# One edge tile in four of layer 0 keeps its messages in one fp32 tensor instead of a high and a low part

## The reference, cut to what matters

```
msg  = relu(x[src] + edge_attr @ W_e + b_e)          # 21250 x 512, edge_attr 21250 x 64
aggr = segment_sum(msg, dst)                         # 1250 x 512
h    = (1 + eps) * x + aggr
h    = silu(batch_norm(h @ W1 + b1)); h = silu(batch_norm(h @ W2 + b2))
x    = layer_norm(x + h)
```

## Time and profile before

| | us |
|---|---|
| median of 3 runs | 876.99 (876.02 to 877.89) |
| the profiled execution, its own time | 880.07 |
| its span, first to last instruction | 878.2 |

### The profile page before, as it was taken

One profiled execution on the slowest core, in us unless ns is written; L12 is line 12 of the kernel. 1 busy time (PEld: TensorE's weight loads), 2 busy tenths in 40 slices (PEclk: granted clock), 3 DMA queues, 4 the chain that ended last, 5 costly groups with the idle time before them and its releaser, 6 DMA issues.

```text
span 878.2 us, 11402 instructions
## 1 busy us (share of the span) xinstructions
PE 793.8 (90%) x3714; PEld 628.5 (72%) x3714; DVE 655.6 (75%) x1161; ACT 450.3 (51%) x805; POOL 349.9 (40%) x381
## 2 busy tenths in 40 slices
PE   7398999898969999969679999999999999999993
PEld 6265655555539999958358888878767798989893
DVE  6379999999997973268569999999985362525365
ACT  4377888888864432211157778778753121111122
POOL 6356677777700000011487777777720000000001
PEclk8789999999999999979789999999999999999996
DMA  8759888888820031003668888888831210100011
GB/s 222 261 157 324 262 245 256 251 251 252 265 95 1 1 121 72 1 12 128 204 191 248 264 257 259 263 256 262 263 100 36 72 72 1 72 1 1 1 49 69
DMA packets 49293, 134.38 MB, mean 153 GB/s; under 512 B 8169, under 2 KB 8425, under 8 KB 48848
## 3 DMA queue, kind: packets, MB, share of 16 engines
q0 software_dynamic: 26720, 87.58, 33.1%
q1 hardware_dynamic: 22020, 45.59, 15.2%
q10 hardware_dynamic: 492, 0.45, 0.2%
HBM read 128.47 MB, written 5.12 MB: 152 GB/s over the span
## 4 chain that ended last, share of the span: by engine, by line
PE 62%; DVE 24%; issue 6%; DMA 4%; ACT 2%; POOL 1%; SPq 0%; DVEq 0%; ACTq 0%; POOLq 0%
PE banks L499 36%; PE banks L526 12%; DVE msg_lo L1085 8%; DVE raw L1093 5%; PE banks L552 4%; PE banks L553 4%; DVE attr_hl L1008 3%; DVE hot L1079 3%; DMA attr_sb<-in_attr 2%; DVE agg L1108 1%; PE banks L566 1%; DVE stats L1209 1%; DMA raw<-table_dram,src_sb 1%; PE banks L575 1%; POOL raw L428 1%
## 5 line engine op out<-in xcount | busy, mean ns | idle before, releaser
L428 POOL DMA_INDIRECT raw<-in_x,src_sb x167 | 159.0, 952 | 80.6 <-DVE msg_lo L1085 50.2
L428 POOL DMA_INDIRECT raw<-table_dram,src_sb x167 | 163.0, 976 | 63.7 <-issue 35.8
L552 PE MATMUL banks<-msg_hi,hot 128*128 128x512 f32 x334 | 142.0, 425 | 9.5 <-DVE msg_lo L1085 7.0
L450 POOL TENSOR_TENSOR moments<-moments,minus_half 128x1 f32<-128x1 f32 x32 | 20.3, 635 | 322.7 <-DVE moments L1215 322.7
L869 ACT ACTIVATE msg_hi<-raw 128x512 fp32r<-128x512 f32 x168 | 105.5, 628 | 69.2 <-DVE raw L1093 67.4
L553 PE MATMUL banks<-msg_lo,hot 128*128 128x512 f32 x334 | 132.6, 397 | 0.0
L1093 DVE TENSOR_TENSOR raw<-banks,raw 128x512 f32<-128x512 f32 x168 | 114.2, 680 | 16.1 <-PE banks L526 12.8
L1085 DVE SCALAR_TENSOR_TENSOR msg_lo<-banks,msg_hi 128x512 fp32r<-128x512 f32 x166 | 112.7, 679 | 15.8 <-ACT msg_hi L869 15.8
L830 ACT ACTIVATE banks<-raw 128x512 f32<-128x512 f32 x166 | 98.7, 595 | 44.5 <-DMA raw<-table_dram,src_sb 36.6
L1085 DVE SCALAR_TENSOR_TENSOR msg_lo<-raw,msg_hi 128x512 fp32r<-128x512 f32 x168 | 113.7, 677 | 3.3 <-ACT msg_hi L869 3.3
L552 PEld LDWEIGHTS banks<-msg_hi,hot 128*128 128x128 f32 x334 | 63.8, 191 | 52.6 <-DVE msg_lo L1085 42.9
(11 more groups left out here) (167 smaller groups left out, 1650.9 us busy)
## 6 DMA issues: line engine op xcount, KB each, us to landing
attr_sb<-in_attr SPq DMA_DIRECT2D x84, 128.0 KB, 4.6
attr_sb<-in_attr SPq DMA_DIRECT2D x42, 256.0 KB, 3.9
Wg_raw<-in_Wg SPq DMA_DIRECT2D x3, 1536.0 KB, 6.5
W_raw<-in_W SPq DMA_DIRECT2D x2, 2048.0 KB, 14.1
raw<-in_x,src_sb POOLq DMA_INDIRECT x167, 4.3
raw<-table_dram,src_sb POOLq DMA_INDIRECT x167, 4.1
x_in<-in_x SPq DMA_DIRECT2D x5, 512.0 KB, 10.4
rows<-in_x SPq DMA_DIRECT2D x1, 2560.0 KB, 12.4
```

What stands on the lines that cost most here:

```text
L428: pool.indirect_dma_start(rows_of(L, t), None, tables[L], bass.IndirectOffsetOnAxis(ap=src_sb[:, t:t + 1], axis=0)).then_inc(gathered[t % ...
L552: nc.tensor.matmul(acc, h, msg_hi[L][:, t % MSG, :], start=start, stop=False)
```

## The change

In layer 0, tiles 3, 7, 11, ... 163 (t % 4 == 3, 41 of 167, all of them odd) become "whole". ACT writes their relu as plain fp32 into `msg_whole`, which lies on the same bytes as layer 0's `msg_hi` and uses the same slots. DVE computes no low part for them. PE sums them with one product on fp32 operands, `hot` read as fp32, where it made two on fp32r operands. Semaphore `low` counts only the tiles that have a low part, and whoever waited for a whole tile's low part (`place` and `sum_product`) waits for its relu (`relued`). The waits of `gather` name even tiles, so their counts change and not what they wait for. Layer 1 is as before.

```
+        msg_whole = at("msg_whole", [P, MSG, D], F32, B0 + 68 * KB)
...
+        def whole(L, t):
+            return L == 0 and t % 4 == 3
+        def lows(L, tiles):
+            return len([t for t in range(tiles) if not whole(L, t)])
...
-                    pool.wait_ge(low[L], t - RAW + 1)
+                    pool.wait_ge(low[L], lows(L, t - RAW + 1))
...
-                pe.wait_ge(low[L], t + 1)
+                if whole(L, t):
+                    pe.wait_ge(relued[L], t + 1)
+                else:
+                    pe.wait_ge(low[L], lows(L, t + 1))
...
-                nc.tensor.matmul(acc, h, msg_hi[L][:, t % MSG, :], start=start, stop=False)
-                mm = nc.tensor.matmul(acc, h, msg_lo[L][:, t % MSG, :], start=False, stop=stop)
+                if whole(L, t):
+                    mm = nc.tensor.matmul(acc, h.bitcast(F32), msg_whole[:, t % MSG, :], start=start, stop=stop)
+                else:
+                    nc.tensor.matmul(acc, h, msg_hi[L][:, t % MSG, :], start=start, stop=False)
+                    mm = nc.tensor.matmul(acc, h, msg_lo[L][:, t % MSG, :], start=False, stop=stop)
...
-                    act.wait_ge(low[L], t - 2 * PLACE_BANKS + 1)
+                    last = t - 2 * PLACE_BANKS
+                    if whole(L, last):
+                        act.wait_ge(relued[L], last + 1)
+                    else:
+                        act.wait_ge(low[L], lows(L, last + 1))
...
+                to = msg_whole if whole(L, t) else msg_hi[L]
+                nc.scalar.activation(to[:, t % MSG, :], edge_bank(t) if odd(t) else rows_of(L, t),
...
-                        if 0 <= t < TILES:
+                        if 0 <= t < TILES and not whole(L, t):
                             low_message(L, t)
```

More of the change, by code:

```diff
@@ L868, in message_high @@
                 wait(act, summed[L], t - MSG + 1)
-                nc.scalar.activation(msg_hi[L][:, t % MSG, :], edge_bank(t) if odd(t) else rows_of(L, t),
+                to = msg_whole if whole(L, t) else msg_hi[L]
+                nc.scalar.activation(to[:, t % MSG, :], edge_bank(t) if odd(t) else rows_of(L, t),
                                      ACT.Relu).then_inc(relued[L], 1)
```

## The result

The changed kernel takes **870.93 us** (median of 6 runs, 866.74 to 872.91) where the kernel before, timed beside it, takes 877.3 (872.71 to 878.27): a ratio of 0.9926 with a 95% interval of 0.9901 to 0.995. It is faster by 6.4 us; 13.5 us were forecast, and 870.9 lies above the upper end of the range.

The account below looks back on a forecast made before the run. DVE was taken to bound layer 0's edge loop, POOL's gathers next. Gathers 8.4 us earlier plus a shorter end made 14.1; less 0.6, 13.5 off the median 876.99 gave 863.5 us, range 860.5 to 869.5.

Parts of the forecast that it names:

- DVE bounds the loop before: Layer 0's edge loop: DVE sets the pace at 1.31 us a tile, 1.16 after the change, and other engines wait.
- PE's product at 0.88 us: A whole tile's sum on PE: one fp32 product of 512 columns costs 0.88 us where two fp32r products cost 0.47.
- the three rivals on PE's price: Layer 0's loop: PE dearer (866 to 870 us, chance 0.12), PE full (873, 0.04), PE the bound (891, 0.05).
- 116 x 1.25 = 145.0: POOL's gathers, tile 50 to 166: 1.25 us each instead of 1.314, so the last gather starts 8.4 us earlier.
- layer 1's period: Layer 1's gathers: 15.16 us for 12 tiles instead of 15.0; used in layer 0, it would take off 1.6 us.
- The last gather to the last low part, 10.0 us: End of layer 0's loop: 10.0 us, from layer 1's 10.6 less one low part, where it was 15.7.
- Where the gain can begin: Layer 0 from about 85 us: tile 50's gather starts at 87.1 instead of 88.11, about 1.0 us earlier.
- The profile stands for the median: The 13.5 us gain read from the profiled execution (880.07 us) was taken off the median, 876.99 us.
- 14.1 forecast: Layer 0's last low part ends at 242.1 instead of 256.2 us, 14.1 us earlier, before 0.6 us is taken off.
- The rest after layer 0 moved unchanged: Everything behind layer 0's edge loop moves with the loop's end, with no change of its own.
- the gather rate falls: Rival, layer 0's loop: transfers stretch and land late, about 8 us gained less delays, 869 to 873 us; chance 0.05.
- ACT's `place` does wait for them: Sign in the second part of layer 0's loop: ACT's `place` waits for gathers, as in layer 1; no size given.

Follow-up runs that it names:

- before_d: The kernel before, unchanged, run again for a second profile without the long common pauses: 875.84 us, ratio 0.999.
- after_c: The changed kernel, run again on another chip without the long common pauses: 871.08 us, ratio 0.9935 to the kernel before.
- port_free_c: Changed kernel with one SBUF operand of DVE's one-hots, features' and even tiles' low parts read from idle PSUM (sums not the reference's): 866.04 us, ratio 0.9893.
- third and fourth sets: Follow-up runs with at most one common pause each: kernels before and after, variants of whole tiles, DVE operands and load order; medians 865.81 to 883.57 us.
- odd2: Changed kernel with all odd tiles of layer 0 whole, 83 instead of 41: 957.45 us (ratio 0.986) with pauses, 883.57 us (1.0083) without.

## Why the prediction was wrong

The pair `before_d` and `after_c` fits for the account: their starts differ by 0.24 us only, their times by 875.60 - 871.57 = 4.0 us, and the medians by 5.2 beside each other. Timelines of ACT, POOL and DVE, first of `before_d`, then of `after_c`:

```profile
36.42 0.63 ACT L830 ACTIVATE attr_hl<-attr_sb 128x512 fp32r<-128x512 f32 x1 [11.24 <-DMA attr_sb<-in_attr]
...
83.53 0.95 POOL L428 DMA_INDIRECT raw<-in_x,src_sb  x1 [0.34 <-DVE msg_lo L1085]
...
235.71 0.94 POOL L428 DMA_INDIRECT raw<-in_x,src_sb  x1 [0.35 <-DVE msg_lo L1085]
...
250.71 0.68 DVE L1085 SCALAR_TENSOR_TENSOR msg_lo<-raw,msg_hi 128x512 fp32r<-128x512 f32 x1
```

```profile
36.66 0.63 ACT L845 ACTIVATE attr_hl<-attr_sb 128x512 fp32r<-128x512 f32 x1 [10.81 <-DMA attr_sb<-in_attr]
...
83.45 1.14 POOL L437 DMA_INDIRECT raw<-in_x,src_sb  x1 [0.30 <-issue]
...
235.23 0.95 POOL L437 DMA_INDIRECT raw<-in_x,src_sb  x1 [0.31 <-issue]
...
245.92 0.68 DVE L1105 SCALAR_TENSOR_TENSOR msg_lo<-raw,msg_hi 128x512 fp32r<-128x512 f32 x1
```

The last gather starts 0.5 us earlier, and that is all that the gathers gained; the last low part ends 4.8 us earlier. From the wait's end to the last low part it is 214.97 us in the one and 209.94 in the other, **5.0 us** less. 4.3 of it is the stock of messages that DVE no longer leaves behind the gathers: 11.4 us instead of 15.7 from the last gather to the last low part. The rate of the gathers, which was to bring 7.4 us, brought 0.4, and 0.3 lie ahead of tile 50's gather.

Step by step:

- *DVE bounds the loop before.* Right. Relieved of 41 low parts, it leaves the gathers free: POOL's waits for its low parts from 62 to 220 us fell from 23.6 to 0.3 us.
- *PE's product at 0.88 us.* Right, 0.87; the three rivals on PE's price fall.
- *"116 x 1.25 = 145.0".* **This is the step that failed.** It held that a gather costs POOL 1.25 us whether or not anything held it up; the rows behind it were all taken where DVE paced the gathers. There they never began inside one of DVE's two-SBUF instructions. Once they run free they do, and 30 to 35 of the 116 are lengthened: 150.04 and 151.78 us, 5.0 and 6.8 us more. The sign stood in the earlier trace rows: two gathers of 1.13 and 1.15 us in layer 1, one in each group. In the trace of the kernel before, 15 gathers of layer 1's loop take over 0.98 us, and every one began inside an even tile's low part, these two 0.36 and 0.34 us after its start. The prediction used them for layer 1's period (15.16 us instead of 15.0) and as 1.6 us that might be taken off, without asking what makes a gather of 0.95 us take 1.15, nor whether layer 0, with an unlike mix on DVE, meets it more often than once in a group.
- *The last gather to the last low part, 10.0 us.* Mis-sized: 12.3 in the profiled execution, 11.4 in `after_c` and in `port_free_c`. It was taken from layer 1 less one low part. A gather of layer 0 lands later, which would make 0.6 of the 1.4 us; that it is the cause is not shown. The page's median from issue to landing in `after_c`:

```profile
raw<-in_x,src_sb POOLq DMA_INDIRECT x167, 4.7
raw<-table_dram,src_sb POOLq DMA_INDIRECT x167, 4.1
```

- *"Where the gain can begin": tile 50's gather 1.0 us earlier.* Between the wait's end and this gather it is 47.11 us in `before_d`, 46.79 in `after_c`: 0.3 us, and not 1.0.
- *The profile stands for the median.* The distance from the wait's end to the last low part is 217.0 us in the first trace of before and 215.0 in the second; the sum started from the longer one. That is 2.0 us of the miss that no trace of the change could show.

Together: 14.1 forecast; less 6.8 for the port and 1.4 for the end; 1.1 more for tile 50's gather, which came 46.8 us behind the wait in `after_c` and not 87.1 - 39.17 = 47.9; less 2.0 for the first trace of before. That leaves 5.0 us, what the pair shows. With the port's excess gone, the term that failed holds: 145.05 us in `port_free_c` for the 145.0. The whole distance fits too, 237.61 - 34.91 = 202.7 us from the wait's end to the last low part where the prediction has 242.1 - 39.17 = 202.9, but by two errors that cancel: 1.6 us less to tile 50's gather (46.3 for 47.9) and 1.4 more at the end.

The rest after layer 0 moved unchanged, as said: from the last low part to the end of the execution it is 623.9 us in the first trace of before, 623.8 in the first of after, and 624.1 to 625.6 in those of the table of the third and fourth sets.

Among the rivals, "the gather rate falls" gave the nearest time (869 to 873) for another reason: I had transfers in mind that land late. ACT's `place` does wait for them, as the prediction said (20.8 us between 83 and 236 us of `after_c`, none before), but `port_free_c` moves the same bytes faster, with 13.9 us of such waits, and loses nothing.

## What to carry to other kernels

When an engine that paced a stream is relieved, the stream can lose the phase that kept it clear of shared resources: take the cost of its steps from a stretch where it already runs free, and ask of every step there that is longer than the rest what it lay beside. If GpSimd issues gathers without a pause, let DVE's two-operand steps beside them read one operand from PSUM, and if some of DVE's work can go, let it be the steps that read SBUF twice. Compare distances from a common event within two executions before the difference of two profiles is taken for the gain.

## What the runs showed of the hardware

- A gather of 128 rows that POOL issues in layer 0's loop takes 0.945 us, and up to 1.47 us when it begins inside a DVE instruction with two SBUF operands; most of what is left of that instruction is added. The same instruction with one PSUM operand adds nothing (0 of 192 gathers in the three kernels with that edit). A one-hot compare and a 64-partition subtraction count as much as a low part. A DVE instruction that begins while a gather is under way isn't held up (107 in `before_d`). One gather of layer 1 took 1.63 us (`after_c`, at 457.07) and began during an add, 0.14 us ahead of an even tile's low part; that is not explained.
- An fp32 product of 512 columns is two records and takes PE 0.87 us, where two fp32r products of the size take 0.47.
- The same kernel took 876 us and 965 us on one chip at different times, with common pauses of PE, ACT and DVE of up to 4 us in the second case, for which the trace names no cause. On such a loop a change worth 5 us read as 0.5 and 3.9, and one that costs 7 us (`odd2`) read as a gain of 13.
